# First narrow attention of a four-layer kernel: shares applied to the outputs, shift of the scores on GpSimd, scores waiting bank by bank

## The chip, the cores and the metric

One core of one Trainium2 chip. The metric is the device time of one execution in microseconds (us), the median over runs; smaller is better. Engines: TensorE (PE, with its weight loads PEld), VectorE (DVE), ScalarE (ACT), GpSimd (POOL), SyncE (SP). Each works through its own instructions in order and meets the others at semaphores.

## What is computed

Four layers on x (2 x 1024 x 256, float32), each a gated cross-attention to a context of 77 rows per batch and a gated feed-forward part. The change touches the attentions of layers 2 and 3, with 16 heads of 16 columns. What layer 2 computes, cut from the reference:

```python
def _L2_xattn_ref(values, keys, queries, mask, Wv, Wk, Wq, Wo, bo):
    ...
    energy = jnp.einsum('nqhd,nkhd->nhqk', q, k)
    energy = jnp.where(mask == 0, jnp.float32(-1e+20), energy)
    attention = jax.nn.softmax(energy / np.sqrt(EMBED).astype(np.float32), axis=3)
    out = jnp.einsum('nhql,nlhd->nqhd', attention, v).reshape(N, q_len, EMBED)
    return out @ Wo.T + bo
```

Layer 3 computes the same without a mask and with biases on queries, keys and values. Layers 0 and 1 have wider heads and their own functions (pe_wide and its like).

## The kernel before

Tiles are of 128 rows of x, NT = 16 of them. A tile's scores are 128 x 1232 (16 heads x 77 context rows) and fill three banks of PSUM; two such sets alternate, and so do two buffers prob in SBUF. The stage of layer 2 is called with n = 5 ("attention 5" below), that of layer 3 with n = 6 ("attention 6"). Both go through pe_attention, act_attention, dve_attention and pool_attention, one function for each engine, each a loop over the tiles t in program order. Only the order inside each engine's function and the semaphores set the order of the work.

One tile of attention 5, by its steps:
- TensorE: scores (L727) once the turned and normalised tile is copied; it also waits for p_kept, the copies of the probabilities of tile t-2, since these lie in the same banks.
- VectorE: adds the mask's bias (L922, PSUM to prob), maximum of each head (dve_softmax, L613), subtracts it (L615, semaphore shifted), then after_shift(): the tile t+2 is normalised (L267), residuals of two earlier tiles are added (L900) on odd t, their statistics (L910) are taken on even t. Then it waits for powered, sums (L620) and takes the reciprocal (L623, semaphore shares_made).
- ACT: exp (L860, semaphore powered); copies of the turned probabilities (L844, L847), of the turned tile (L825), and of the weighed outputs of a pair of tiles (keep_outputs, L835).
- GpSimd: multiplies the probabilities by the reciprocals (L983, semaphore weights_made), then adds the gated bias to x (L985). after(t) follows: pool_root at t = 4, 8, 12, 15 (L243 and what follows it), and pool_order at t = 12. Ahead of its first tile stands pool_group_rows of the stage before (L2144 to L2152).
- TensorE again: turns the probabilities (L395) after weights_made, weighs the values by pairs of tiles (L742, function weigh), and multiplies by the output weights (L751, function outputs). weigh(u) also waits for the residuals of the pair before, because they use the same bank.

At t = 2 of attention 5, before(t) on VectorE handles four tiles of the stage before ("gated rows", L1962, two inputs in SBUF, each followed by L1965), ahead of the normalisation. At the end of attention 5 the rows for the next stage are fed: dve_feed_rows (L267), pe_feed_turn, act_feed_copy (L1634), pe_feed_product (L1627) and the tables (L2304, L2309 and after), and the first experts' matrices follow.

Attention 6 already does it otherwise. It has no bias, VectorE reads the scores from PSUM, and the reciprocals are not multiplied into the probabilities: GpSimd spreads them over 256 columns (L990), TensorE turns them (L382), ACT copies them (keep_shares, L856), and VectorE multiplies the weighed outputs of a pair by them (divided_outputs, L905). There TensorE also makes the queries (L712), which ACT copies (L830).

Of the kernel before, what the change touches and what calls it, by code (L numbers as in the profile page):

```python
# [64 lines left out]
def build(nc, ctx, a, out):  # L65
# [313 lines left out]
    def pe_turn_shares(pe, t):  # L379
        pe.wait_ge(weights_made, 6 * NT + t + 1)  # L380
        for g in range(KD):
            ins = pe.transpose(shares_bank(t)[:, g * P:(g + 1) * P],  # L382
                               wide_shares[:, t % 2, :, :].rearrange("p h c -> p (h c)")[:, g * P:(g + 1) * P], ident[:, :])
        return ins

    def pe_turn_probabilities(pe, n, t):
        g, base = NT * n + t, t % 2 * 3 * BANK
        if n == 6:
            pe.wait_ge(powered, g + 1)
        else:  # L390
            pe.wait_ge(weights_made, g + 1)
        for b0 in range(0, CH, 4):
# [4 lines left out]
            if n == 6 and t >= 1 and b0 + 4 >= CH:  # L397
                ins = pe_turn_shares(pe, t - 1)
# [209 lines left out]
    def dve_softmax(dve, n, t, src, after_shift, divide=True):  # L608
# [4 lines left out]
        dve.tensor_reduce(negmax, src, AX.X, ALU.max, negate=True).then_inc(dve_step, 1)  # L613
        dve.wait_ge(dve_step, vs())
        dve.tensor_tensor(Pb, src, negmax.unsqueeze(2).to_broadcast([P, H, S2]), ALU.add).then_inc(shifted, 1)  # L615
        after_shift()
        dve.wait_ge(powered, g + 1)
        if n == 6 and t >= 2:
            dve.wait_ge(weights_made, g - 1)
        dve.tensor_reduce(total, Pb, AX.X, ALU.add).then_inc(dve_step, 1)  # L620
        dve.wait_ge(dve_step, vs())
        if not divide:
            dve.reciprocal(total, total).then_inc(shares_made, 1)  # L623
            return
# [44 lines left out]
    wide_shares = prep[:, 8704:9216].rearrange("p (n h c) -> p n h c", n=2, c=HD)  # L669
    shares_T = prep[:, 7680:8704].rearrange("p (n g i q) -> p n g i q", n=2, g=KD, i=2)  # L670
# [25 lines left out]
    def pe_attention(pe, n, wo, w_query=None, feed=False):  # L696
# [19 lines left out]
        def scores(t):  # L716
# [5 lines left out]
            if t >= 2:  # L722
                pe.wait_ge(p_kept, 3 * (g0 + t - 1))
            for bank in NARROW:
# [7 lines left out]
        def weigh(u, halves=(0, 1)):  # L732

            bt, turned_pair, bank = 2 * u // TB, pair_probT[u % 2], weighed_bank(u)
            if halves[0] == 0:
                pe.wait_ge(p_kept, 3 * (g0 + 2 * u + 2))
# [33 lines left out]
        for t in range(NT):  # L770
# [5 lines left out]
            if feed:  # L776
# [6 lines left out]
                if t == NT - 2:  # L783
                    pe_feed_turn(pe, 0)
                    pe.wait_ge(p_kept, 3 * (g0 + t + 1))
# [32 lines left out]
    def act_attention(act, n, scale, q_bias=None, feed=False):  # L818
# [14 lines left out]
        def keep_outputs(u):  # L833
            act.wait_ge(weighed, g0 + 2 * u + 2)
            act.copy(outT[:, :, :].rearrange("p g c -> p (g c)"), weighed_bank(u)).then_inc(outputs_kept, 1)  # L835

        def keep_probabilities(t):
# [3 lines left out]
            for b0 in range(0, CH, 4):  # L841
                m = min(4, CH - 1 - b0)
                act.wait_ge(p_turned, 3 * (g0 + t) + b0 // 4 + 1)
# [2887 lines left out]
```

## Time and profile before

| | |
|---|---|
| median of 3 runs | 3222.62 us (3219.43 to 3229.44) |
| the profiled execution | 3226.4 us, span 3225.1 us |
| busy share of the span | PE 94%, PEld 69%, DVE 66%, ACT 38%, POOL 26% |
| attention 5 | about 2024.5 to 2163 us of the span |
| attention 6 | about 2420 to 2549 us of the span |
| granted TensorE clock, mean | 0.978 of full speed |

Times in the rows are microseconds from the start of the span, and durations in microseconds unless a row says otherwise. A timeline row with x2 or more holds neighbouring instructions of the same kind, with the time of all of them; in square brackets stands the idle time before it and what ended it. The busy share of TensorE comes from pipelined matmuls, so 94% doesn't mean that it works at its peak.

### The profile page before, as it was taken

The numbers are of one execution on the slowest core, as the hardware profiler recorded it, in microseconds if no ns is written. First come the engines' busy times: TensorE is split into PE (matmuls) and PEld (weight loads), VectorE is DVE, ScalarE is ACT, GpSimd is POOL, SyncE is SP. The second block draws the span as 40 slices with busy tenths as digits, with TensorE's granted clock in tenths as the row PEclk, the third lists the DMA queues.
The fourth block names the chain that finished last, engine by engine and source line by source line (L and its number), as shares of the span: only waits on it lengthen the run. The fifth ranks groups of instructions, "written<-read, shape, count | busy, mean of one in ns | idle before, by whom it ended". The sixth has DMA issues, their size and how long they took to land.

```text
span 3225.1 us, 43512 instructions
## 1 busy us (share of the span) xinstructions
PE 3036.0 (94%) x16352; PEld 2228.9 (69%) x16352; DVE 2137.6 (66%) x3877; ACT 1224.5 (38%) x2349; POOL 850.8 (26%) x1286
## 2 busy tenths in 40 slices
PE   7999999999999999999999999789999899997996
PEld 5678877667767776777699999565666655555664
DVE  5996879567855885686478887883228667764113
ACT  4343332553355335432233333331225345662331
POOL 1306500100110020001246655440443221111554
PEclk9999999999999999999999999999999999997998
DMA  5200100010002000200032221002550011112633
GB/s 137 67 1 1 29 27 1 13 42 27 1 14 68 0 1 14 67 1 1 14 92 79 87 85 53 20 1 105 211 198 1 21 34 51 33 39 103 217 124 108
DMA packets 104614, 176.42 MB, mean 55 GB/s; under 512 B 27125, under 2 KB 75799, under 8 KB 99671
## 3 DMA queue, kind: packets, MB, share of 16 engines
q1 hardware_dynamic: 89527, 102.32, 10.2%
q0 software_dynamic: 14880, 71.33, 6.2%
q8 instruction: 132, 2.16, 0.3%
q14 instruction: 75, 0.61, 0.1%
HBM read 198.31 MB, written 17.56 MB: 67 GB/s over the span
## 4 chain that ended last, share of the span: by engine, by line
PE 75%; DVE 13%; ACT 4%; issue 3%; POOL 2%; DMA 2%; SPq 0%; DVEq 0%; ACTq 0%; POOLq 0%
PE psum L419 9%; PE psum L442 8%; PE psum L1393 7%; PE psum L1405 6%; PE psum L2527 6%; PE psum L1874 5%; PE psum L1829 5%; PE psum L2548 3%; PE psum L409 2%; PE psum L455 2%; PE psum L1114 2%; PE psum L2703 2%; PE psum L3128 2%; DVE row L620 1%; DVE psum L3386 1%
## 5 line engine op out<-in xcount | busy, mean ns | idle before, releaser
L419 PE MATMUL psum<-Vt,shared 128*128 128x256 f32 (+1 forms) x1600 | 361.7, 381 | 0.4
L442 PE MATMUL psum<-Kt,xnTt 128*128 128x512 f32 (+1 forms) x960 | 343.9, 508 | 0.5 <-ACT xnTt L527 0.5
L419 PEld LDWEIGHTS psum<-Vt,shared 128*128 128x128 f32 (+1 forms) x1600 | 297.8, 190 | 39.3 <-issue 1.2
L442 PEld LDWEIGHTS psum<-Kt,xnTt 128*128 128x128 f32 x960 | 179.9, 190 | 158.0 <-issue 153.1
L1405 PEld LDWEIGHTS psum<-expert_w,prep 128*128 128x128 f32 x1024 | 194.6, 190 | 77.7 <-issue 57.4
L245 POOL TENSOR_SCALAR root_v<-meanvar 128x8 f32<-128x8 f32 (+3 forms) x19 | 8.6, 455 | 903.7 <-DVE meanvar L223 903.7
L3386 DVE CUSTOM_DVE_ANT_0 psum<-psum,expert_w 128x128 f32<-128x128 f32 (+7 forms) x256 | 191.8, 775 | 76.5 <-PE psum L3128 73.3
L1405 PE MATMUL psum<-expert_w,prep 128*128 128x256 f32 x1024 | 240.8, 379 | 0.0
L1393 PE MATMUL psum<-weights,expert_w 128*128 128x512 f32 x512 | 240.3, 593 | 0.0
L1319 DVE SCALAR_TENSOR_TENSOR bias<-Kt,small,bias 128x1232 f32<-128x1232 f32 x96 | 149.1, 1554 | 129.8 <-ACT Kt L1303 128.5
L620 DVE TENSOR_REDUCE row<-shared 128x16 f32<-128x1232 f32 x112 | 160.5, 1433 | 81.5 <-ACT shared L536 70.0
L3275 ACT ACTIVATE prep<-psum 128x512 f32<-128x512 f32 (+3 forms) x384 | 167.2, 493 | 108.0 <-PE psum L3151 107.1
L2620 DVE TENSOR_TENSOR prep<-psum,prep 128x512 f32<-128x512 f32 x62 | 42.8, 691 | 210.3 <-PE psum L2527 193.7
L1448 ACT ACTIVATE prep<-psum,bias 128x512 f32<-128x512 f32 x128 | 88.0, 688 | 237.2 <-PE psum L1393 237.2
L536 ACT ACTIVATE shared<-shared 128x1232 f32<-128x1232 f32 x80 | 98.5, 1232 | 186.8 <-DVE shared L615 186.8
L647 DVE TENSOR_TENSOR shared<-psum,bias 128x1232 f32<-128x1232 f32 x80 | 115.0, 1437 | 70.5 <-PE psum L442 65.4
L1393 PEld LDWEIGHTS psum<-weights,expert_w 128*128 128x128 f32 x512 | 96.1, 190 | 69.1 <-issue 63.1
L615 DVE TENSOR_TENSOR shared<-shared,row 128x1232 f32<-128x1232 f32 x96 | 140.9, 1467 | 3.3
L613 DVE TENSOR_REDUCE row<-shared 128x16 f32<-128x1232 f32 x96 | 137.8, 1436 | 3.3
L527 ACT COPY xnTt<-psum 128x256 f32<-128x256 f32 x80 | 29.3, 374 | 288.1 <-PE psum L365 288.1
L1303 ACT ACTIVATE Kt<-fside,small 128x1232 f32<-128x1232 f32 x96 | 134.4, 1403 | 1.5 <-DVE bias L1319 1.5
L3128 PE MATMUL psum<-weights 72*128 72x512 bf16 (+3 forms) x384 | 106.8, 335 | 19.8 <-DVE row L3386 17.1
(510 smaller groups left out, 6636.5 us busy)
## 6 DMA issues: line engine op xcount, KB each, us to landing
weights<-in_L_ffn_w SPq DMA_DIRECT2D x32, 512.0 KB, 4.7
expert_w<-in_L_ffn_w SPq DMA_DIRECT2D x32, 512.0 KB, 4.5
expert_w<-in_L_xattn_Wf SPq DMA_DIRECT2D x16, 512.0 KB, 5.9
weights<-q_parts SPq DMA_DIRECT2D x32, 144.0 KB
weights<-k_parts SPq DMA_DIRECT2D x96, 48.0 KB
weights<-in_L_xattn_Wk SPq DMA_DIRECT2D x4, 1024.0 KB, 4.9
weights<-in_L_xattn_Wv SPq DMA_DIRECT2D x4, 1024.0 KB, 7.0
weights<-in_L_xattn_Wq SPq DMA_DIRECT2D x4, 1024.0 KB, 5.3
```

Of the source, the lines that this page charges most:

```text
L419: ins = pe.matmul(o_bank(t), probT[0:rows, t % 2, c, :], Vt[0:rows, t // TB, c, :], start=(c == 8), stop=(c == 7))
L442: ins = pe.matmul(flat[:, par * 3 * BANK + at:par * 3 * BANK + at + cols], xnTt[:, par, k, :], Kt[:, t // TB, k, src:src + cols], start=(k ...
L620: dve.tensor_reduce(total, Pb, AX.X, ALU.add).then_inc(dve_step, 1)
L1319: dve.scalar_tensor_tensor(flat_bias, hinge[:, j % 2, :], wto[:, j:j + 1], flat_bias, ALU.mult, ALU.add).then_inc(hinge_added, 1)
L1393: ins = pe.matmul(bank, slot(s)[0][:, k, f * P:(f + 1) * P], xnT_of(g)[:, k, :], start=(k == 0), stop=(k == KD - 1))
L1405: ins = pe.matmul(y[:, t * D:(t + 1) * D], hidden[:, n % 4, t * P:(t + 1) * P], slot(s)[2][:, f, :], start=(n % GROUP_STEPS == 0 and t % 2 ...
L1829: return pe.matmul(product_of(i), lhs, rhs, start=start, stop=stop, skip_group_check=True)
L1874: ins = pe.matmul(acc_of(i)[:, t * P:(t + 1) * P], lhs[:, t * P:(t + 1) * P], rhs, start=(begin and start and t == 0), stop=end, skip_grou ...
L2527: ins = pe.matmul(psum[:, 2 * (c % 2) + n, :], rows_xT[:, c % 2, k, :], w[:, at:at + F], start=(k == 0), stop=(k == KD - 1))
L3128: ins = pe.matmul(flat[:, base + at:base + at + w], heads[0:STACK, 0, s, t * P:(t + 1) * P], heads[0:STACK, 1, s, at:at + w], start=True, ...
L3275: act.activation(expT[:, h % 2, to:to + w], psum[:, ring_bank(("piece", h, i)), 0:w], ACT.Exp, scale=float(HD3) ** -0.5).then_inc(exp_made, 1)
L3386: dve.tensor_tensor_reduce(flat[:, base:base + cols], flat[:, base:base + cols], later[:, S - cols:S], 1.0, -3.0e38, ALU.add, ALU.max, max ...
```

## The change

Attention 5 takes over the way of attention 6 for the shares: no multiplication of the probabilities; the reciprocals are spread, turned, copied, and multiplied into the outputs of a pair by VectorE. On ACT, keep_outputs goes, keep_shares comes. TensorE turns the probabilities after powered. VectorE's L615 goes from attention 5, and GpSimd does the shift, signalled by the maximum over the semaphore row_made, which counts two per tile in attention 5 (maximum and reciprocal). In both attentions TensorE's scores wait bank by bank for the copied chunks of tile t-2 and no longer once for all three. The shares of attention 5 lie in a part of Vt that is free by then. tiles_turned(n, t) counts the turns and copies of the tiles before t: three per tile, and one more behind attention 5's last tile. The diff, cut:

```diff
@@ pe_turn_shares, pe_turn_probabilities @@
-        if n == 6:
-            pe.wait_ge(powered, g + 1)
-        else:
-            pe.wait_ge(weights_made, g + 1)
+        pe.wait_ge(powered, g + 1)
...
-            if n == 6 and t >= 1 and b0 + 4 >= CH:
-                ins = pe_turn_shares(pe, t - 1)
+            if t >= 1 and b0 + 4 >= CH:
+                ins = pe_turn_shares(pe, n, t - 1)
@@ dve_softmax @@
-        dve.tensor_reduce(negmax, src, AX.X, ALU.max, negate=True).then_inc(dve_step, 1)
-        dve.wait_ge(dve_step, vs())
-        dve.tensor_tensor(Pb, src, negmax.unsqueeze(2).to_broadcast([P, H, S2]), ALU.add).then_inc(shifted, 1)
+        if n == 5:
+            dve.tensor_reduce(negmax, src, AX.X, ALU.max, negate=True).then_inc(row_made, 1)
+        else:
+            dve.tensor_reduce(negmax, src, AX.X, ALU.max, negate=True).then_inc(dve_step, 1)
+            dve.wait_ge(dve_step, vs())
+            dve.tensor_tensor(Pb, src, negmax.unsqueeze(2).to_broadcast([P, H, S2]), ALU.add).then_inc(shifted, 1)
         after_shift()
         dve.wait_ge(powered, g + 1)
-        if n == 6 and t >= 2:
+        if n >= 5 and t >= 2:
             dve.wait_ge(weights_made, g - 1)
...
+    def tiles_turned(n, t):
+
+        return 3 * (NT * n + t) + n - 5
@@ pe_attention @@
-            if t >= 2:
-                pe.wait_ge(p_kept, 3 * (g0 + t - 1))
-            for bank in NARROW:
+            for i, bank in enumerate(NARROW):
+                if t >= 2:
+                    pe.wait_ge(p_kept, tiles_turned(n, t - 2) + i + 1)
...
         if feed:
             pe_tables(pe)
-        else:
-            pe_turn_shares(pe, NT - 1).then_inc(p_turned, 1)
+            pe.wait_ge(xt_fed, 2)
+        pe_turn_shares(pe, n, NT - 1).then_inc(p_turned, 1)
         weigh(PAIRS - 1)
         if feed:
             pe_feed_turn(pe, 2)
-            pe.wait_ge(xt_fed, 2)
         outputs(PAIRS - 1)
@@ act_attention @@
-        def keep_outputs(u):
-            act.wait_ge(weighed, g0 + 2 * u + 2)
-            act.copy(outT[:, :, :].rearrange("p g c -> p (g c)"), weighed_bank(u)).then_inc(outputs_kept, 1)
...
-                    if not feed and t >= 1:
+                    if t >= 1:
                         ins = keep_shares(t - 1)
@@ dve_attention, after_shift @@
                 before(t)
                 if biased:
+                    if t % 2 == 0 and t >= 4:
+                        divided_outputs(t // 2 - 2)
                     if t + 2 < NT:
                         dve_normed(dve, n, x, t + 2)
                     if t % 2 and t >= 5:
                         residual(t - 5)
                         residual(t - 4)
+                    if t == NT - 1:
+                        divided_outputs(PAIRS - 2)
...
         for u in range(PAIRS - 3 if biased else PAIRS - 2, PAIRS):
-            if not biased:
+            if not biased or u == PAIRS - 1:
                 divided_outputs(u)
@@ pool_attention @@
             if n == 5:
-                pool.wait_ge(shares_made, NT * (n - 5) + t + 1)
-                pool.tensor_tensor(Pb, Pb, shares.to_broadcast([P, H, S2]), ALU.mult).then_inc(weights_made, 1)
+                Pb = prob[:, par, :].rearrange("p (h c) -> p h c", h=H)
+                pool.wait_ge(row_made, 2 * t + 1)
+                pool.tensor_tensor(Pb, Pb, negmax.to_broadcast([P, H, S2]), ALU.add).then_inc(shifted, 1)
             pool.wait_ge(normed, NT * n + t + 1)
             pool.tensor_tensor(x[:, t, :], x[:, t, :], gated_bo, ALU.add).then_inc(bo_added, 1)
-            if n == 6:
-                pool.wait_ge(shares_made, NT * (n - 5) + t + 1)
-                if t >= 2:
-                    pool.wait_ge(p_turned, 3 * (NT * n + t))
-                pool.tensor_copy(wide_shares[:, par, :, :], shares.to_broadcast([P, H, HD])).then_inc(weights_made, 1)
+            pool.wait_ge(row_made, 2 * t + 2 if n == 5 else 2 * NT + t + 1)
+            if t >= 2:
+                pool.wait_ge(p_turned, tiles_turned(n, t))
+            pool.tensor_copy(wide_shares(n)[:, par, :, :], shares.to_broadcast([P, H, HD])).then_inc(weights_made, 1)
             if after:
                 after(t)
```

## Rows read from the trace of the kernel before

**Rows 1.** Page, part 1: busy us (share of the span) and instructions per engine.
```profile
PE 3036.0 (94%) x16352; PEld 2228.9 (69%) x16352; DVE 2137.6 (66%) x3877; ACT 1224.5 (38%) x2349; POOL 850.8 (26%) x1286
```

**Rows 2.** Chain of waits in attention 5: start us, us, what.
```profile
2097.23 2.26 POOL shared L983
...
2101.55 1.26 ACT shared L860
...
2102.84 1.45 DVE row L620
```

**Rows 3.** Timeline, tiles 14 and 15 of attention 5: start us, us, engine, line, operation.
```profile
2139.73 1.44 DVE L620 TENSOR_REDUCE row<-shared 128x16 f32<-128x1232 f32 x1
...
2141.20 0.25 DVE L623 RECIPROCAL row<-row 128x16 f32<-128x16 f32 x1
2141.37 1.38 DVE L922 TENSOR_TENSOR shared<-psum,bias 128x1232 f32<-128x1232 f32 x1
2141.53 2.25 POOL L983 TENSOR_TENSOR shared<-shared,row 128x1232 f32<-128x1232 f32 x1 [4.42 <-DVE row L623]
2142.78 1.44 DVE L613 TENSOR_REDUCE row<-shared 128x16 f32<-128x1232 f32 x1
...
2144.25 1.51 DVE L615 TENSOR_TENSOR shared<-shared,row 128x1232 f32<-128x1232 f32 x1
...
2145.69 0.86 DVE L900 SCALAR_TENSOR_TENSOR x<-psum,tanh_g,x 128x256 f32<-128x256 f32 x2
```

**Rows 4.** Busy time by stretches, mid-stage: us, each engine's busy us, PEclk, DMA.
```profile
2059.00:2133.84 74.84, 59.89 (x416) 39.52 (x414) 70.71 (x87) 31.90 (x65) 39.27 (x47) 1.00 0.00 1
```

**Rows 5.** Waits in attention 6: engine, line, releaser: us in total, times, longest.
```profile
PE psum L727 <- ACT prep L856: 6.0, 7, 1.0
```

**Rows 6.** Timeline, the first three tiles of attention 5.
```profile
2033.25 2.36 POOL L2152 TENSOR_TENSOR prep<-prep,fside 128x1024 f32<-128x1024 f32 x1
...
2034.79 1.38 DVE L922 TENSOR_TENSOR shared<-psum,bias 128x1232 f32<-128x1232 f32 x1
...
2047.08 0.47 DVE L1962 SCALAR_TENSOR_TENSOR x<-prep,gates,x 128x256 f32<-128x256 f32 x1
...
2052.81 1.38 DVE L922 TENSOR_TENSOR shared<-psum,bias 128x1232 f32<-128x1232 f32 x1
```

**Rows 7.** Timeline, one odd tile of attention 6.
```profile
2477.66 0.40 DVE L267 TENSOR_SCALAR xn<-x,meanvar,rstd 128x256 f32<-128x256 f32 x1
...
2480.69 0.69 DVE L905 TENSOR_TENSOR prep<-psum,prep 128x512 f32<-128x512 f32 x1
...
2480.89 1.24 ACT L844 COPY prep<-psum 128x512 f32<-128x512 f32 x3
...
2481.48 0.38 PE L365 MATMUL psum<-ident,xn 128*128 128x128 f32 x2
...
2482.69 2.36 PE L727 MATMUL psum<-Kt,qTt 128*128 128x512 f32 x8 [0.83 <-ACT prep L856]
```

**Rows 8.** Timeline, the end of attention 5.
```profile
2146.70 2.32 PE L742 MATMUL psum<-shared,Vt 128*32 128x256 f32 x34 [1.55 <-DVE x L900]
...
2148.78 2.58 DVE L267 TENSOR_SCALAR inner<-x,meanvar,rstd 128x256 f32<-128x256 f32 x2
2148.94 2.26 POOL L983 TENSOR_TENSOR shared<-shared,row 128x1232 f32<-128x1232 f32 x1 [4.47 <-DVE row L623]
```

**Rows 9.** Line 2149 over the whole run: duration ns min/median/max, first and last start us.
```profile
L2149 POOL TENSOR_TENSOR prep<-expert_w x4: 731/734/1927, 1733.4 to 2030.5; 128x256 f32<-128x256 f32 x4
```

**Rows 10.** Timeline of GpSimd after tile 12 of attention 5.
```profile
2129.78 1.30 POOL L243 TENSOR_SCALAR root_v<-meanvar 128x4 f32<-128x4 f32 x1
...
2133.52 0.29 POOL L2227 TENSOR_SCALAR_AFFINE_SELECT small<-ones 128x128 f32<-128x128 f32 x1
```

**Rows 11.** Two stretches of attention 5, columns as in group 4.
```profile
2044.00:2045.00 1.00, 0.00 (x0) 0.00 (x0) 0.96 (x2) 0.00 (x0) 1.00 (x1) 1.00 0.00 0
2048.00:2049.00 1.00, 1.00 (x2) 0.48 (x3) 0.97 (x4) 0.93 (x1) 0.00 (x0) 0.50 0.00 0
```

More of the change, by code:

```diff
@@ L622, in dve_softmax @@
         if not divide:
-            dve.reciprocal(total, total).then_inc(shares_made, 1)
+            dve.reciprocal(total, total).then_inc(row_made, 1)
             return
@@ L668, in build, with wide_shares, shares_T @@
     HD = D // H
-    wide_shares = prep[:, 8704:9216].rearrange("p (n h c) -> p n h c", n=2, c=HD)
-    shares_T = prep[:, 7680:8704].rearrange("p (n g i q) -> p n g i q", n=2, g=KD, i=2)
+    def wide_shares(n):
+        at = flat_V1[:, 3840:4352] if n == 5 else prep[:, 8704:9216]
+        return at.rearrange("p (n h c) -> p n h c", n=2, c=HD)
+    def shares_T(n):
+        at = flat_V1[:, 2816:3840] if n == 5 else prep[:, 7680:8704]
+        return at.rearrange("p (n g i q) -> p n g i q", n=2, g=KD, i=2)
+    def tiles_turned(n, t):
+        return 3 * (NT * n + t) + n - 5
     def shares_bank(t):
@@ L735, in weigh @@
             if halves[0] == 0:
-                pe.wait_ge(p_kept, 3 * (g0 + 2 * u + 2))
+                pe.wait_ge(p_kept, tiles_turned(n, 2 * u + 2))
                 if u >= 1 and u < PAIRS - 1:
@@ L855, in keep_shares @@
                 act.wait_ge(outputs_kept, PAIRS * (n - 5) + u - 1)
-            return act.copy(shares_T[:, u % 2, :, t % 2, :], shares_bank(t).rearrange("p (g q) -> p g q", g=KD))
+            return act.copy(shares_T(n)[:, u % 2, :, t % 2, :], shares_bank(t).rearrange("p (g q) -> p g q", g=KD))
         def power(t):
@@ L876, in act_attention @@
                 keep_tile(t + 3)
-            if feed and t % 2 == 0 and t >= 2:
-                keep_outputs(t // 2 - 1)
             if q_bias is not None and t + 3 < NT:
@@ L883, in act_attention @@
                     act_feed_copy(act, i)
+        act.wait_ge(p_turned, tiles_turned(n, NT) + 1)
+        keep_shares(NT - 1).then_inc(p_kept, 1)
         if feed:
-            keep_outputs(PAIRS - 1)
             for i in range(2, FEED_PAIRS):
                 act_feed_copy(act, i)
-        else:
-            act.wait_ge(p_turned, 3 * (g0 + NT) + 1)
-            keep_shares(NT - 1).then_inc(p_kept, 1)
     def dve_attention(dve, n, biased, gate, before, after, feed=False):
@@ L903, in divided_outputs @@
             dve.wait_ge(weighed, g0 + 2 * u + 2)
-            dve.wait_ge(p_kept, 3 * (g0 + 2 * u + 2) + (3 if u < PAIRS - 1 else 1))
+            dve.wait_ge(p_kept, tiles_turned(n, 2 * u + 2) + (3 if u < PAIRS - 1 else 1))
             dve.tensor_tensor(outT[:, :, :].rearrange("p g c -> p (g c)"), weighed_bank(u),
-                              shares_T[:, u % 2, :, :, :].rearrange("p g i q -> p (g i q)"), ALU.mult).then_inc(outputs_kept, 1)
+                              shares_T(n)[:, u % 2, :, :, :].rearrange("p g i q -> p (g i q)"), ALU.mult).then_inc(outputs_kept, 1)
         def statistics(t):
@@ L918, in dve_attention @@
             if t >= 2:
-                dve.wait_ge(p_turned, 3 * (g0 + t - 1))
+                dve.wait_ge(p_turned, tiles_turned(n, t - 1))
             if biased:
@@ L971, in dve_attention @@
                 dve_tables(dve)
-    shares_made = sem("shares_made")
+    row_made = sem("row_made")
     def pool_attention(pool, n, gated_bo, after=None):
@@ L978, in pool_attention @@
             par = t % 2
-            Pb = prob[:, par, :].rearrange("p (h c) -> p h c", h=H)
-            shares = row[:, par, H:2 * H].unsqueeze(2)
+            negmax, shares = (row[:, par, i * H:(i + 1) * H].unsqueeze(2) for i in range(2))
             if n == 5:
-                pool.wait_ge(shares_made, NT * (n - 5) + t + 1)
-                pool.tensor_tensor(Pb, Pb, shares.to_broadcast([P, H, S2]), ALU.mult).then_inc(weights_made, 1)
+                Pb = prob[:, par, :].rearrange("p (h c) -> p h c", h=H)
+                pool.wait_ge(row_made, 2 * t + 1)
+                pool.tensor_tensor(Pb, Pb, negmax.to_broadcast([P, H, S2]), ALU.add).then_inc(shifted, 1)
             pool.wait_ge(normed, NT * n + t + 1)
             pool.tensor_tensor(x[:, t, :], x[:, t, :], gated_bo, ALU.add).then_inc(bo_added, 1)
-            if n == 6:
-                pool.wait_ge(shares_made, NT * (n - 5) + t + 1)
-                if t >= 2:
-                    pool.wait_ge(p_turned, 3 * (NT * n + t))
-                pool.tensor_copy(wide_shares[:, par, :, :], shares.to_broadcast([P, H, HD])).then_inc(weights_made, 1)
+            pool.wait_ge(row_made, 2 * t + 2 if n == 5 else 2 * NT + t + 1)
+            if t >= 2:
+                pool.wait_ge(p_turned, tiles_turned(n, t))
+            pool.tensor_copy(wide_shares(n)[:, par, :, :], shares.to_broadcast([P, H, HD])).then_inc(weights_made, 1)
             if after:
```

10 lines of the change are left out of this document (5 added, 5 removed).

## The prediction

> **What bounds the kernel now.** I read the page first (shares and slices), then the chain of waits over the two narrow attentions, then the timeline of single tiles in them. The page has TensorE busy 94% of the span [rows 1], so only a stage where TensorE is not the last to arrive can be moved by work on other engines. The first narrow attention (attention 5) is such a stage. Its chain of waits goes round once a tile without touching TensorE for long: GpSimd's multiplication, transposes and copies, exp of the next tile, row sum, reciprocal, and GpSimd again; transposes and copies have the 2.06 us between 2099.49 and 2101.55 [rows 2]. VectorE is nearly full besides: in one tile [rows 3] bias add 1.38, maximum 1.44, shift 1.51, then 0.40 of normalising or its like and 0.86 of residuals, sum 1.44, reciprocal 0.25, together 7.3 us; over ten tiles it was busy 70.71 of 74.84 us, 94% [rows 4]. Two limits of the same size, so taking away one alone gives nothing.
>
> The second narrow attention (attention 6) is bound by TensorE. The waits list shows TensorE's scores waiting 6.0 us in 7 pieces for ACT's copy of the shares (L856) [rows 5]: the second thing that the change can move.
>
> **What the change does in attention 5, per tile.** Call T the end of the maximum L613. Removed: VectorE's shift (1.51) and GpSimd's multiplication by the shares. Added on GpSimd: the shift, 128x1232 in place with a row of 16 broadcast, which is the shape of the multiplication it replaces, so 2.25 us [rows 3]. Its other end is the plain two-tensor add L2152, 2.36 us for 1024 columns [rows 6], so 2.84 for 1232; I take 2.25, since shape and broadcast are the same, and nothing there suggests less. GpSimd also makes the widened shares (a copy of 256 columns, put at 0.4 to 0.5), VectorE multiplies outputs once a pair (0.69, L905) [rows 7], TensorE turns the shares, two transposes a tile, and ACT copies them instead of the outputs.
>
> What matters is the order on VectorE, which has one queue. dve_softmax still does maximum, after_shift(), wait for powered, sum. Before, shift and after_shift work filled VectorE, and only exp (1.26) had to be covered. Now exp(t) waits for GpSimd's shift(t), and VectorE can't go to tile t+1 meanwhile. From T to the sum: hand-over 0.08 (as from L623 at 2141.20+0.25 to L983 at 2141.53), shift 2.25, exp 1.26, and hand-overs of 0.05 and 0.03 (as from exp's end at 2102.81 to the sum at 2102.84): 3.67 us [rows 2, 3]. Then sum to next bias add 1.48 + 0.17, and bias add to T 1.41 + 1.44 (starts at 2139.73, 2141.20, 2141.37, 2142.78) [rows 3]. **New period 3.67 + 1.65 + 2.85 = 8.17 us a tile**, all serial, against (2141.37 - 2052.81)/12 = 7.38 [rows 3, 6].
>
> Everything else of the change lies in the 3.67 us in which VectorE waits. On odd tiles that is a norm of 0.40 [rows 7] and two residuals 0.86; on even ones the divided outputs 0.69, a norm and two statistics of about 0.4 each. In even tiles the norm comes while GpSimd's shift is running, and the trace shows what that does: two norms of 2.58 us (L267, 2148.78) beside a GpSimd multiplication from 2148.94 to 2151.20 [rows 8], against about 0.7 for two. The second waited until GpSimd was done. So the norm ends at T+2.5 and the statistics at T+3.3, still under 3.67. If this cover failed (0.4 us more in it), the tile would grow by what is over.
> The Trainium skill, SBUF — State Buffer, section "SBUF: two separate sides", says that a VectorE instruction in a two-port mode or with two SBUF inputs and a GpSimd instruction hold a shared port pair exclusively, the other blocking fully; the trace agrees (2.58 us above). Without such a lock tile 2 below would cost 1.85 us less and the forecast would fall by that.
>
> TensorE was busy 59.89 of the 74.84 us [rows 4], 11.8 us a pair of tiles; four more transposes, about 0.5 us, make 12.3 of the new 16.3, so it follows. In the new order it waits for the norm of an even tile (T+2.5) and has an idle stretch of about 3 us each pair.
>
> **The sum for attention 5**, in the trace's own times.
> - Tile 0. GpSimd's shift stands behind pool_group_rows, which ends with L2152 at 2033.25+2.36 = 2035.6. One of its adds, L2149, took 1.93 against a median of 0.73 [rows 9] (it ran beside the VectorE shift L615, which is gone), so the queue is free at 2034.4. Shift to 2036.7, exp to 2038.0, then 0.03+1.48+0.17: bias add of tile 1 at 2039.7, where it was at 2034.79 [rows 6]. **+4.9**. Before, VectorE's shift did not care about this queue.
> - Tiles 1 and 2. Tile 1 takes 8.17 (2047.9), T of tile 2 is 2050.7. There before() runs the gated rows (L1962, two SBUF inputs, four times). From the first of them to the next bias add it is 5.73 us (2052.81 - 2047.08) [rows 6]; GpSimd's shift gets in after the first one and holds the second back: ready at T+0.86, free at T+2.7, 1.85 more. Bias add of tile 3 at 2058.3 against 2052.81: **+5.5** up to here.
> - Tiles 3 to 14: 12 x 8.17 = 98.0 against 88.6: **+9.5**.
> - GpSimd's roots, in after(t) at t = 4, 8 and 12, stand between the widened shares and the next shift. At t = 12 root and order take from 2129.78 to 2133.81, of which L243 has 1.30 where about 0.2 is usual (it met a VectorE shift) [rows 10], so 3.0; with 0.5 for the copy before it, it ends 3.5 after the reciprocal, and the shift is wanted at 2.85: 0.65 late. The shorter ones 0.15 each: **+1.0**. They had 4.4 us of slack before.
> - Tail. The residuals that weigh(6) waits for follow the maximum at once, 1.5 us sooner than before (L900 at 2145.69, L742 at 2146.70) [rows 3, 8], but the last division on VectorE stands behind three sets of feed rows, a root and dve_tables, so outputs(7) come at about the same distance from T as they did. The wait for xt_fed 2 moves ahead of the last shares and weigh(7), but pe_feed_product(1), before it in TensorE's order, has waited for the same value: nothing. Ahead of weigh(6) TensorE now idles some 4 us and may find a lower clock: 0 to +3.5, I take **+1**.
> Together 5.5+9.5+1.0+1 = **+17**.
>
> **Attention 6.** scores(t+2) now wait bank by bank. On odd t TensorE has nothing between the turned tile (L365, until 2481.86) and the scores L727 at 2482.69, although the first copy L844 (from 2480.89, about 0.6) was done at 2481.5 [rows 7]. The first bank's matmuls then take 0.9 us, by which the second copy is there, and the third bank comes after 1.9 us, when the shares' copy is long over. So each 0.83 to 0.97 goes. The next in line, exp and norm, have a microsecond and more. 7 of them are **-6**; bounds 0 (another wait steps in) and -7. In attention 5 the same wait (0.92 per tile) goes as well and is worth nothing there, since TensorE isn't last.
>
> Net +17 - 6 = +11. The profiled execution took 3226.4 us, which gives 3237.4; the median of the three runs is 3222.6, 3.8 lower, so **3233.6**.
>
> **Rivals.**
> 1. *VectorE's relief counts* (faster). If VectorE's busy time were the limit, a tile would lose 1.51 and gain 0.35 (0.69 a pair): that is 15 x 1.16 = 17 us off, and with attention 6 -23: 3199. For it: VectorE was 94% busy [rows 4]. Against: it decides by whether VectorE has 3.67 us of work between maximum and sum; it has 1.3 to 1.9. Break-even with the old 7.38 is at 2.88, which GpSimd's 2.25 alone plus exp exceeds. 0.06.
> 2. *Bank by bank gives nothing in attention 6*: 3222.6 + 17 = 3240. It needs TensorE to be held by the query copy or exp instead. 0.12.
> 3. *GpSimd's add is dear*: 2.84 instead of 2.25, 15 x 0.59 = +9: 3242. 0.10.
> The Trainium skill, GPSIMD Engine Reference, section 4.1 "Engine selection", speaks against this change: two-input elementwise work is about 2x slower on GpSimd than on VectorE. That would be 2 x 1.51 = 3.0 us, an estimate by this page, for +11 more (3245); the multiplication row has 2.25, which is 1.5x, and so far the trace does not agree.
> 4. *The clock of TensorE falls in attention 5.* After TensorE idled from 2042.7 to 2045.2, the granted clock went to 0.50 (1.2 GHz), and was there at 2048 to 2049 [rows 11]. The new idle stretch of 3 us per pair is like it. At half clock every TensorE step takes twice as long; by my schedule seven microseconds of that per pair leave the scores 0.7 us ahead of VectorE, and three more would make each of 7 pairs 1.5 us longer: +10, 3244. 0.13.
> 5. *A kinder clock later*: the stage's last part and the expert stage after it begin at half clock, and another timing could spare about 5 us: 3228. 0.11.
> The likeliest, the sum as reckoned, 0.48: 3229 to 3238.
>
> **Chances.** 0.3% is about what a measurement of this kernel can tell from no change: 9.7 us, so the line is at 3232.3, just under the forecast. Of the likeliest case I put 0.30 above it and 0.18 below. Slower 0.30 + 0.12 + 0.10 + 0.13 = 0.65; same 0.18 + 0.11 = 0.29; faster 0.06. The range goes from the kinder clock less 2 us to the dear end of rivals 3 and 4: 3226 to 3246; left out are rival 1 and the cases where two dear ones meet.
>
> **What would show it.** In the profile after: bias add to bias add (the former L922) 8.1 to 8.3 us in mid-stage; VectorE's sum preceded by 1.5 to 2.3 us of idle released by ACT on odd tiles and by little on even ones; the chain of waits as VectorE, GpSimd, ACT, VectorE; GpSimd's shift at 2.25; a norm of over 2 us in even tiles; the first shift near 2034.5; in attention 6 no wait of L727 for L856, and the stage 6 us shorter. The prediction is wrong if the period stays below 7.6, if the shift takes over 2.5, or if TensorE's rows in attention 5 are doubled for long.

## The result, and the profile after

The changed kernel takes 3231.68 us (median of 19 runs, 3225.48 to 3235.29) where the kernel before, run beside it, takes 3223.06 (19 runs, 3215.46 to 3232.89). The ratio is 1.0027, with a 95% interval of 1.0019 to 1.0035: 8.6 us slower, where 11.0 were forecast. The sign is sure; the size is just under the line of 0.3% above which the prediction called the change slower, and the interval reaches over that line. The profiled execution took 3231.02 us against 3226.4 before. In this section I read it by stages, since what attention 5 lost and attention 6 gave back are both larger than the net.

Page of the kernel after, part 1 (busy us, share of the span, instructions):

```profile
PE 3034.7 (94%) x16384; PEld 2232.7 (69%) x16384; DVE 2126.9 (66%) x3869; ACT 1223.3 (38%) x2357; POOL 852.2 (26%) x1302
```

Beside [rows 1] VectorE has 10.7 us less to do and GpSimd 1.4 us more. Nothing in this view tells that the kernel became slower. The timeline of two tiles in mid-stage does (kernel after; VectorE, GpSimd and ACT; start us, us, engine, line, operation, and in brackets the idle time before it and what ended it):

```profile
2098.27 1.44 DVE L620 TENSOR_REDUCE row<-shared 128x16 f32<-128x1232 f32 x1 [2.61 <-ACT shared L865]
2099.74 0.25 DVE L623 RECIPROCAL row<-row 128x16 f32<-128x16 f32 x1
...
2099.91 1.38 DVE L923 TENSOR_TENSOR shared<-psum,bias 128x1232 f32<-128x1232 f32 x1
...
2101.33 1.44 DVE L611 TENSOR_REDUCE row<-shared 128x16 f32<-128x1232 f32 x1
...
2102.68 0.68 DVE L906 TENSOR_TENSOR prep<-psum,Vt 128x512 f32<-128x512 f32 x1
...
2102.84 2.25 POOL L988 TENSOR_TENSOR shared<-shared,row 128x1232 f32<-128x1232 f32 x1 [2.38 <-DVE row L611]
...
2103.28 1.96 DVE L267 TENSOR_SCALAR xn<-x,meanvar,rstd 128x256 f32<-128x256 f32 x1
...
2105.12 1.23 ACT L865 ACTIVATE shared<-shared 128x1232 f32<-128x1232 f32 x1 [3.01 <-POOL shared L988]
2105.16 0.74 DVE L911 BATCH_NORM_STATS2 bn<-x 128x6 f32<-128x256 f32 x2
...
2106.39 1.44 DVE L620 TENSOR_REDUCE row<-shared 128x16 f32<-128x1232 f32 x1
...
2108.02 1.38 DVE L923 TENSOR_TENSOR shared<-psum,bias 128x1232 f32<-128x1232 f32 x1
```

From one bias add (L923) to the next it is 8.11 us (2099.91 to 2108.02), where [rows 3, 6] gave 7.38. The maximum L611 ends at 2102.77, the row sum L620 starts at 2106.39: 3.62 us, filled by GpSimd's shift (2.25) and ACT's exp (1.23) one behind the other. VectorE has one queue, and the sum stands in it ahead of the next tile's bias add. The sum of the tile before (2098.27) shows the same from the other side: VectorE idle for 2.61 us until exp was done. The chain of waits of the kernel after, one tile earlier (tile 7), is the whole round, with hand-overs of 0.07 us and less between the engines (start us, us, what):

```profile
2091.70 1.39 DVE shared L923
...
2093.12 1.45 DVE row L611
...
2094.63 2.35 POOL shared L988
...
2097.01 1.24 ACT shared L865
...
2098.27 1.45 DVE row L620
```

Over twelve tiles, in the columns of [rows 4]:

```profile
2058.90:2158.00 99.10, 82.60 (x545) 58.18 (x543) 78.10 (x97) 38.91 (x86) 47.53 (x64) 0.92 0.00 1
```

VectorE is busy 78.10 of 99.10 us, 79%, where it was 94%. The waits list of attention 5 (kernel after, 2025 to 2180; engine, line, releaser: us in total, times, longest) says who keeps whom:

```profile
ACT shared L865 <- POOL shared L988: 57.7, 16, 8.7
...
DVE row L620 <- ACT shared L865: 30.5, 12, 7.2
```

ACT's exp waits for the shift in all 16 tiles, and VectorE's sum for exp in 12 of them; for TensorE's scores VectorE waits in tile 0 alone, as in the kernel before.

The start of the stage, where the forecast saw the largest single loss (kernel after, timeline):

```profile
2033.14 2.35 POOL L2156 TENSOR_TENSOR prep<-prep,fside 128x1024 f32<-128x1024 f32 x1
2035.45 2.25 POOL L988 TENSOR_TENSOR shared<-shared,row 128x1232 f32<-128x1232 f32 x1
...
2038.99 1.44 DVE L620 TENSOR_REDUCE row<-shared 128x16 f32<-128x1232 f32 x1 [7.19 <-ACT shared L865]
...
2040.63 1.38 DVE L923 TENSOR_TENSOR shared<-psum,bias 128x1232 f32<-128x1232 f32 x1
...
2051.77 2.42 POOL L988 TENSOR_TENSOR shared<-shared,row 128x1232 f32<-128x1232 f32 x1 [2.39 <-DVE row L611]
...
2052.46 2.01 DVE L1966 SCALAR_TENSOR_TENSOR x<-prep,gates,x 128x256 f32<-128x256 f32 x1
```

The first shift stands behind the group rows (L2156) and starts at 2035.45; VectorE waits 7.19 us. In tile 2 the second gated row (L1966) takes 2.01 instead of 0.47 [rows 6], until the shift that began before it is done.

In attention 6 the wait of [rows 5] is gone from the waits list. The odd tile's scores now start as soon as TensorE has turned the normed tile, before the copy of the shares (L861) has begun (kernel after, timeline):

```profile
2482.13 0.38 PE L365 MATMUL psum<-ident,xn 128*128 128x128 f32 x2
...
2482.35 2.29 PE L737 MATMUL psum<-Kt,qTt 128*128 128x512 f32 x8
...
2482.73 0.39 ACT L861 COPY prep<-psum 128x256 f32<-128x256 f32 x1
```

The account, from the starts of the same instructions in the two traces (us, after less before):

| stretch | before | after | change |
|---|---|---|---|
| bias add of tile 0 to that of tile 3 | 25.88 | 30.88 | +5.0 |
| bias add of tile 3 to that of tile 15 | 88.56 | 98.89 | +10.3 |
| bias add of tile 15 to the copy of the logits | 32.25 | 30.34 | -1.9 |
| the experts, up to attention 6's first maximum | 251.18 | 251.70 | +0.5 |
| attention 6, up to the next stage's first norm | 124.51 | 118.44 | -6.1 |

The sum is +7.8. Attention 5 began 1.1 us later in this execution, and 4.3 us came back behind attention 6, where nothing was changed (granted clock from 2585 to 2625: 0.83 before, 0.96 after; that the clock is the whole reason is not shown). So the spans differ by 4.7, and the medians by 8.6.

### The profile page after: what moved, and what is told of

Same layout as the page of the kernel before. It is cut to its first block, busy times and chain, and to the rows that moved or that the text cites. A ratio compares the mean times of both kernels' runs of the same rounds, so it can differ in the third digit from the quotient of the medians.

```text
span 3229.8 us, 43628 instructions
## 1 busy us (share of the span) xinstructions
PE 3034.7 (94%) x16384; PEld 2232.7 (69%) x16384; DVE 2126.9 (66%) x3869; ACT 1223.3 (38%) x2357; POOL 852.2 (26%) x1302
## 4 chain that ended last, share of the span: by engine, by line
PE 74%; DVE 14%; issue 4%; ACT 3%; POOL 3%; DMA 1%; SPq 0%; DVEq 0%; POOLq 0%; ACTq 0%
PE psum L416 9%; PE psum L439 8%; PE psum L1397 7%; PE psum L1409 6%; PE psum L2531 6%; PE psum L1878 5%; PE psum L1833 5%; PE psum L2552 3%; PE psum L406 2%; PE psum L452 2%; PE psum L1118 2%; PE psum L2707 2%; DVE row L620 2%; PE psum L3132 2%; DVE psum L3390 1%
## 5 line engine op out<-in xcount | busy, mean ns | idle before, releaser
L620 DVE TENSOR_REDUCE row<-shared 128x16 f32<-128x1232 f32 x112 | 160.5, 1433 | 106.3 <-ACT shared L533 70.0
L533 ACT ACTIVATE shared<-shared 128x1232 f32<-128x1232 f32 x80 | 98.5, 1232 | 187.0 <-DVE shared L615 187.0
L579 ACT COPY shared<-psum 128x512 f32<-128x512 f32 (+1 forms) x240 | 107.4, 482 | 42.9 <-PE psum L406 42.3
L615 DVE TENSOR_TENSOR shared<-shared,row 128x1232 f32<-128x1232 f32 x80 | 116.3, 1454 | 2.8
```

## Experiments

The theory: in attention 5 the new period is one serial round, VectorE, GpSimd, ACT and VectorE again, closed by VectorE's fixed order; the bank-wise wait is a gain of its own in attention 6; the shares on the outputs cost next to nothing. The rivals: TensorE or its clock sets the new period, or the shares do, or the two gains and losses don't simply add.

**One wait instead of three.** The changed kernel, with its scores waiting once for all the copies of the tile's bank:

```
+            if t >= 2:
+                pe.wait_ge(p_kept, tiles_turned(n, t - 2) + 3)
-            for i, bank in enumerate(NARROW):
-                if t >= 2:
-                    pe.wait_ge(p_kept, tiles_turned(n, t - 2) + i + 1)
+            for bank in NARROW:
```

> The changed kernel, but the scores wait once for all three copies of tile t-2, as before. Theory (the serial chain costs attention 5 some 14 us, the waits by bank return 6 in attention 6): the waits of L727's successor for the shares' copy are back in attention 6, 6 us in 7 pieces; attention 6 is 6 us longer than in the changed kernel and like before; attention 5 stays at 8.17 a tile; in all 6 us slower than the changed kernel, 13 to 15 us slower than the kernel before. Rival (waits by bank give nothing in attention 6 and the measured time comes from a smaller loss in attention 5): no difference from the changed kernel, 8 to 9 us slower than before.

Measured: 3237.20 us, ratio to the kernel before 1.0042 (1.0027 to 1.0058), by the medians 14.6 us slower. This interval overlaps that of the changed kernel, so the stage has to show it: attention 6 is back at 124.31 us. Its waits list has the old row again, and the odd tile's scores wait as in [rows 7] (kernel with one wait; waits, then timeline):

```profile
PE psum L737 <- ACT prep L861: 6.0, 7, 1.0
```

```profile
2485.82 2.36 PE L737 MATMUL psum<-Kt,qTt 128*128 128x512 f32 x8 [0.83 <-ACT prep L861]
```

The steps of attention 5 are those of the changed kernel (12.61, 8.21, 10.06, ...). So the wait is worth 6 us in attention 6 and nothing in attention 5.

**The banks alone.** The kernel before, with only the waits by bank:

```
-            if t >= 2:
-                pe.wait_ge(p_kept, 3 * (g0 + t - 1))
-            for bank in NARROW:
+            for i, bank in enumerate(NARROW):
+                if t >= 2:
+                    pe.wait_ge(p_kept, 3 * (g0 + t - 2) + i + 1)
```

> The kernel before with one edit: scores wait bank by bank in both attentions, nothing else. Theory: 6 us faster than before, all of it in attention 6; attention 5 unchanged at 7.38 us a tile, since TensorE is not last there. Rival (the copies are waited for elsewhere next): within 1 us of before.

Measured: 3213.13 us, ratio 0.9972 (0.9961 to 0.9983). Attention 6 takes 118.44 us, the same as in the changed kernel to the hundredth; attention 5 keeps the steps of before, but for one tile (8.03 for 7.41) in which the granted clock fell to 0.50. That is 9.5 us by the medians where the stage gives 6.1; the ratio's interval, 5.5 to 12.6 us, holds both. The two profiled executions are 15.6 us apart, and most of that lies where the code is the same: 3.1 in the end of attention 5, 4.1 in the experts, 3.6 behind attention 6. Whether the edit has a part in these is not shown. For the end of attention 5, 29.13 us from the last bias add to the logits instead of 32.25, the windows show a reason (the kernel before, then banks alone, columns as in [rows 4]; the last but two is the granted clock):

```profile
2169.00:2172.00 3.00, 3.00 (x17) 3.00 (x16) 0.00 (x0) 0.59 (x1) 0.00 (x0) 0.50 0.00 0
```

```profile
2169.00:2172.00 3.00, 3.00 (x28) 3.00 (x28) 0.11 (x1) 1.05 (x2) 0.00 (x0) 1.00 0.02 5
```

From about 2165 to 2182 the one ran at 0.50 (1.2 GHz), the other at 1.00 (2.4 GHz).

**The shift back on VectorE.** The changed kernel with the shares on the outputs and the banks, without the shift on GpSimd:

```
-        if n == 5:
-            dve.tensor_reduce(negmax, src, AX.X, ALU.max, negate=True).then_inc(row_made, 1)
-        else:
...
+        dve.tensor_reduce(negmax, src, AX.X, ALU.max, negate=True).then_inc(dve_step, 1)
+        dve.wait_ge(dve_step, vs())
+        dve.tensor_tensor(Pb, src, negmax.unsqueeze(2).to_broadcast([P, H, S2]), ALU.add).then_inc(shifted, 1)
```

> The changed kernel with the shift of attention 5 back on VectorE; shares stay applied to the outputs. Theory (the loss is the serial link through GpSimd, not the shares): mean of an odd tile 2.85+1.51+1.3+1.65 = 7.3 and an even one 2.85+1.51+1.9+1.65 = 7.9 at most, so 7.3 to 7.6 a tile instead of 8.2, and tile 0's 4.9 us are back; attention 5 about 13 us shorter than in the changed kernel, within 3 us of before; with attention 6 at -6, 3 to 8 us faster than before. Rival (the shares' extra transposes, copies and divisions cost the time): stays near 8.2 a tile and 8 us slower than before.

Measured: 3217.03 us, ratio 0.9986 (0.9974 to 0.9998). The period falls to 7.26 on most tiles and 7.45 to 7.85 on the others, 7.45 in the mean of the last eleven steps against 7.38 before. The place of the long wait is filled (this kernel, timeline):

```profile
2103.72 1.44 DVE L612 TENSOR_TENSOR shared<-shared,row 128x1232 f32<-128x1232 f32 x1
2105.08 0.41 DVE L267 TENSOR_SCALAR xn<-x,meanvar,rstd 128x256 f32<-128x256 f32 x1
2105.41 0.87 DVE L898 SCALAR_TENSOR_TENSOR x<-psum,tanh_g,x 128x256 f32<-128x256 f32 x2
2106.46 1.44 DVE L617 TENSOR_REDUCE row<-shared 128x16 f32<-128x1232 f32 x1 [0.19 <-ACT shared L862]
```

Only exp has to be waited out, and VectorE's own work covers it but for 0.19 us. From the first bias add of attention 5 to the last it is 116.44 us, against 129.77 in the changed kernel and 114.44 before. So of the 15.3 us that the change loses there, 13.3 go with the shift on GpSimd, and 2.0 stay with everything else, the shares on the outputs among it. With the shift undone the change is faster than before, by 5.5 us of the medians.

**The next tile's lead put ahead of the wait.** If it is VectorE's order that closes the round, then bias add and maximum of tile t+1, issued before VectorE waits for exp of tile t, open it, with GpSimd still making every shift:

```
+        if n == 5 and t + 1 < NT:
+            lead(t + 1)
         dve.wait_ge(powered, g + 1)
...
+        def lead(t):
...
+            dve.tensor_tensor(Pb, src, bias[:, t, :].unsqueeze(1).to_broadcast([P, H, S2]), ALU.add).then_inc(dve_step, 1)
+            dve.wait_ge(dve_step, vs())
+            dve.tensor_reduce(row[:, par, 0:H], Pb, AX.X, ALU.max, negate=True).then_inc(row_made, 1)
...
+            if n == 5 and t + 1 < NT:
+                shift(t + 1)
```

(`shift` is GpSimd's wait and its add, made now before it spreads the shares of tile t.)

> The changed kernel, but in attention 5 VectorE makes bias add and maximum of tile t+1 before it waits for tile t's exp, and GpSimd shifts tile t+1 before it spreads the shares of tile t. Nothing is added or left out. Theory (the loss is only that VectorE stands idle over GpSimd's shift and exp): the idle time is filled, VectorE's own work sets 6.1 to 6.3 us a tile, or TensorE a little more (6.3 to 6.7); 15 tiles by 1.7 = 25 us less than the changed kernel, and 3 to 5 more from tile 0's queue: 14 to 22 us faster than before. Rival (GpSimd's or TensorE's work is the limit, or the shared port, VectorE's norms waiting for the shift): 7.4 to 8.2 a tile, not faster than before.

Measured: 3204.65 us, ratio 0.9945 (0.9930 to 0.9959), 18 us below the kernel before and faster than every version without the lead. From tile 4 on the period is 6.1 to 6.4 us (6.7 in the last); the first four tiles take 33.7 us together, 33.2 before. VectorE in one tile, and the stage's windows (kernel with the lead ahead):

```profile
2095.33 0.93 DVE L267 TENSOR_SCALAR xn<-x,meanvar,rstd 128x256 f32<-128x256 f32 x1
2096.18 0.86 DVE L903 SCALAR_TENSOR_TENSOR x<-psum,tanh_g,x 128x256 f32<-128x256 f32 x2
2096.96 1.43 DVE L924 TENSOR_TENSOR shared<-psum,bias 128x1232 f32<-128x1232 f32 x1
2098.42 1.44 DVE L926 TENSOR_REDUCE row<-shared 128x16 f32<-128x1232 f32 x1
2099.77 1.43 DVE L622 TENSOR_REDUCE row<-shared 128x16 f32<-128x1232 f32 x1
...
2103.26 1.44 DVE L924 TENSOR_TENSOR shared<-psum,bias 128x1232 f32<-128x1232 f32 x1 [0.24 <-PE psum L739]
```

```profile
2058.00:2128.00 70.00, 67.81 (x495) 47.47 (x494) 66.07 (x90) 36.25 (x80) 43.22 (x61) 1.00 0.01 1
```

The sum L622 (2099.77) is that of the tile whose maximum was L926 one period earlier; exp has long been done and nothing is waited for. VectorE is 94% busy again, TensorE 97%, and it is TensorE's scores that VectorE waits for now (0.24 us at 2103.26). GpSimd's shift takes what it took (same kernel, timeline):

```profile
2093.86 2.25 POOL L999 TENSOR_TENSOR shared<-shared,row 128x1232 f32<-128x1232 f32 x1 [3.01 <-DVE row L926]
```

**A longer link.** A GpSimd copy of 192 columns before each shift, once in the changed kernel and once in the one with the lead ahead. In a serial round it must show in full, in an open one not. (With the lead ahead the copy also waits for the shift of the tile before, which GpSimd, working in order, has behind it by then.)

```
+    spare = sb("spare", [P, 192])
...
+                pool.tensor_copy(spare[:, :].rearrange("p (h c) -> p h c", h=H), negmax.to_broadcast([P, H, 12]))
```

> The changed kernel with one more small GpSimd copy (128x192, some 0.35 us with its gap, result unused) between the wait for the maximum and the shift of each tile of attention 5. Theory (maximum, shift, exp and sum are one serial chain): every tile grows by the copy, 8.17 to about 8.5, and attention 5 by 14 to 16 times 0.35, 5 to 6 us; about 14 us slower than before. Rival (VectorE's own work or TensorE sets the tile): no change against the changed kernel, since GpSimd is half idle.

> The same extra copy ahead of GpSimd's shift, put into the version in which VectorE runs a tile ahead. Theory (there the chain through GpSimd has slack, since VectorE has work for the whole of shift and exp): 0 to 1 us in attention 5 against that version, though the copy is the same as in the run before; from its rows the shift ends 1.2 us or more before ACT needs it on most tiles. Rival (GpSimd is on the critical path there as well): 5 to 6 us.

Measured, changed kernel with the copy: 3231.52 us, ratio 1.0039 (1.0021 to 1.0056). From the first bias add to the last it is 134.62 us instead of 129.77, +4.85. The copy stands between the maximum and the shift (this kernel, timeline):

```profile
2103.21 0.35 POOL L989 COPY spare<-row 128x192 f32<-128x192 f32 x1 [2.37 <-DVE row L611]
2103.52 2.25 POOL L990 TENSOR_TENSOR shared<-shared,row 128x1232 f32<-128x1232 f32 x1
```

Every step has grown by about 0.3 (8.40 for 8.11, 8.52 for 8.21). One has grown by 0.75 (tile 3, 8.96 for 8.21): its exp stood behind ACT's copies of what TensorE had turned late, after a stretch at a granted clock of 0.50. That is the serial round, link by link. By medians alone this can't be told: the kernel is 9.6 us slower than before, where about 14 were expected, the ratio is 1.2 thousandths above that of the changed kernel, and the intervals overlap.

With the lead ahead: 3207.06 us, ratio 0.9959 (0.9943 to 0.9974). Here the expectation missed. The stage grew by 4.2 us from first to last bias add (102.39 to 106.6) where the round's slack should have swallowed nearly all. 1.4 of it is one step (tile 3, 9.46 for 8.02), and that is the clock, not the link: TensorE's 22 matmuls that only keep it at work, ahead of that tile's turning, took 4.90 us instead of 3.81 and the turning 1.64 instead of 1.26, since the granted clock was still at 0.50 (until 2060 here, until 2055 in the other; lead ahead, then with the copy):

```profile
2052.42 3.81 PE L371 MATMUL psum<-ident 128*128 128x128 f32 x22
```

```profile
2054.29 4.90 PE L371 MATMUL psum<-ident 128*128 128x128 f32 x22
```

Of the other 2.8 us, tiles 1 and 2 have 0.3 each and eight of the last eleven tiles 0.23 to 0.29 each, and one instruction shows where from (lead ahead with the copy; compare 2095.33 above, the same tile without it):

```profile
2098.29 2.25 POOL L1002 TENSOR_TENSOR shared<-shared,row 128x1232 f32<-128x1232 f32 x1
```

```profile
2099.47 1.22 DVE L267 TENSOR_SCALAR xn<-x,meanvar,rstd 128x256 f32<-128x256 f32 x1
```

The norm ended at 2100.69, behind the end of the shift (2100.54) by 0.15; without the copy it ended at 2096.26, behind 2096.11 by the same 0.15. Every norm of tiles 3 to 13 ends 0.15 to 0.17 behind the shift, in both kernels. A shift that ends 0.3 later holds VectorE's norm 0.3 longer, though nobody needs the shift yet. The round is open for the data, but not for whatever holds the two engines apart.

**Tile 0's shift on VectorE.** The forecast put +4.9 on tile 0, since the first shift stands behind the group rows on GpSimd:

```
+            if t == 0:
+                dve.wait_ge(row_made, 1)
+                dve.tensor_tensor(Pb, src, negmax.unsqueeze(2).to_broadcast([P, H, S2]), ALU.add).then_inc(shifted, 1)
```

> The changed kernel with the shift of tile 0 alone on VectorE, as before the change. Theory (tile 0's shift stands behind the stage before on GpSimd's queue, 4.9 us by the prediction, 12.60 against 7.86 us from the first bias add to the second in the traces): the first step is 7.9 again, all later ones stay at 8.2; attention 5 is 4.7 us shorter than in the changed kernel, 3 to 4 us slower than before. Rival (the delay would come back at the next tile, whose shift meets the same queue): less than 2 us gained.

> The version in which VectorE runs a tile ahead, and tile 0's shift on VectorE besides. Theory: exp of tile 0 comes at about 6 us after the first bias add and not 10; the scores of tile 2, for which VectorE waited 3.2 us, come as much earlier; 3 to 4 us less in attention 5 than without, so 20 to 22 us faster than before. Rival (GpSimd's queue holds tile 1's shift instead, or the 4 gated rows take the gain): within 1 us of the version without.

Measured, in the changed kernel: 3225.83 us, ratio 1.0012 (1.0003 to 1.0022). First to last bias add 125.25 us, 4.52 less than in the changed kernel; the first step is 7.85 as before, 4.7 less, and the others stay (8.21, 10.06, 8.11) but for the fourth (8.46 for 8.21). That is the queue's price, alone. By the medians the kernel is 3.9 us slower than before, as expected (3 to 4).

Measured, with the lead ahead: 3203.28 us, ratio 0.9934 (0.9921 to 0.9948). This missed what the theory gave it: the stage is 0.5 us shorter (101.88 for 102.39), not 3 to 4. Exp of tile 0 did end early, 6.2 us after the first bias add. But the second bias add comes 5.58 us after the first where it was 3.69, since the shift stands ahead of it on VectorE, and the third, 15.11 us after the first where it was 16.15, had to wait (this kernel, TensorE and VectorE):

```profile
2033.93 4.90 PE L371 MATMUL psum<-ident 128*128 128x128 f32 x22
2038.62 1.71 PE L392 MATMUL psum<-ident,shared 128*128 128x128 f32 x10
...
```

```profile
2042.84 1.44 DVE L924 TENSOR_TENSOR shared<-psum,bias 128x1232 f32<-128x1232 f32 x1 [3.38 <-PE psum L739]
```

The 22 matmuls that only keep TensorE at work (L371, from pe_stay_at_work) took 4.90 us; for tile 0 of the changed kernel and of the one with the lead ahead they took 2.62. Here they began later, behind a norm that stood behind the shift on VectorE, after TensorE had done 0.56 us of work in 4, and ran at half clock (this kernel, windows):

```profile
2030.00:2034.00 4.00, 0.56 (x3) 0.56 (x4) 3.96 (x4) 1.23 (x1) 3.90 (x4) 0.84 0.00 0
2034.00:2038.50 4.50, 4.50 (x23) 4.50 (x23) 4.43 (x5) 0.37 (x1) 4.44 (x3) 0.50 0.21 25
```

So tile 0 was turned from 2038.62, behind them in TensorE's order, 10.9 us after the first bias add, where GpSimd's late shift had it at 11.0 (2037.12 less 2026.11). What VectorE had won, TensorE no longer had, and the scores of tile 2 (L739) had VectorE wait 3.38 us. The time of the two kernels can't be told apart (intervals 0.9921 to 0.9948 and 0.9930 to 0.9959).

## Why the prediction was right

The sign, the place and the mechanism were right; the sum came out 2.4 us high by the medians, and 3.7 high by the stages of the two traces (11.0 for 7.3), of which the tail has 2.9. The chances did less well: the prediction gave 0.65 to a ratio above its line of 0.3%, with its forecast 1.3 us over that line, and the measured 0.27% lies under it.

*The period.* Forecast 8.17, measured 8.11 on even tiles and 8.21 on odd ones from tile 3 on, where no root stands before the shift. Each link is where it was put: shift 2.25, exp 1.23, hand-overs of 0.07, 0.03 and 0.04. The 0.10 of the odd tiles is a thing the forecast didn't have: VectorE's norm of 0.40 is still running when the shift begins, and the shift takes 2.35 (2094.63 in the chain above). The argument that removing VectorE's 1.51 buys nothing, since VectorE has to wait for what took its place, is what the shift on VectorE (7.45) and the lead ahead (6.1) show from two sides. The idle before the sum on odd tiles is 2.6 to 3.4 us, not 1.5 to 2.3. That range doesn't follow from the prediction's own terms, which leave 2.4 (0.40 and 0.86 of 3.67); nor does the work of up to 1.9 us that its first rival gives VectorE there.

*Start of the stage.* +5.5 forecast, +5.0 measured: tile 0 is +4.7 (forecast 4.9), by the kernel with tile 0's shift on VectorE 4.5; the first shift was due at 2034.5 and began at 2035.45, in a stage that began 1.1 late. The second gated row (L1966) was held to 2.01, 1.5 us more where 1.85 were forecast, and tile 2 took no longer than before (10.07 for 10.05): VectorE's own shift of 1.51 is gone from it, and the length of the gated rows hides GpSimd's shift and exp.

*Roots.* +1.0 forecast. The steps behind them are those of the odd tiles 5, 9 and 13, 8.36, 8.36 and 8.86 against 8.21 on odd tiles without a root: 0.15, 0.15 and 0.65, each as forecast. Tiles 3 to 14 came to 98.89 us where period and roots together gave 99.0.

*Norm beside the shift.* 1.96 us in even tiles (a pair of them 2.04 at 2153.71) instead of 0.40, and covered: it ends at 2105.24, exp at 2106.35. The cover is thin where statistics are gathered as well: VectorE was idle ahead of the sum for 0.49 us in tile 6, but for 0.07 in tiles 8 and 12. The Trainium skill, SBUF — State Buffer, section "SBUF: two separate sides", says that a VectorE instruction in a two-port mode, or with two SBUF inputs, blocks until a GpSimd instruction that started first is done, and the other way round. The traces agree here, in the 0.93 and 1.22 of the lead-ahead kernels and in the 2.35 of the odd tiles' shift; that the norm is in such a mode no run shows.

*The price of GpSimd's add.* 2.25, so the rival of 2.84 is out. The Trainium skill, GPSIMD Engine Reference, section 4.1 "Engine selection", has two-input work at about twice VectorE's time; the trace has 2.25 against 1.44 to 1.51, 1.5 to 1.6 times, and the measurement decides.

*Attention 6.* -6 forecast, -6.1 measured, and given back by one wait to within 0.2. The eight kernels that wait by bank have 118.4 to 120.5 us there, the two that wait once 124.3 and 124.5.

*The tail.* This is the term that was off: +1 forecast, -1.9 measured. What was foreseen did happen. TensorE idled 3.87 us ahead of weigh(6) and came back slower (kernel after, timeline; 2.32 us in [rows 8]):

```profile
2161.58 3.16 PE L752 MATMUL psum<-shared,Vt 128*32 128x256 f32 x34 [3.87 <-DVE x L901]
```

But the kernel before had itself run at 0.50 from 2165 to 2182, where the kernel after was at full clock from 2166 to 2186 and at 0.50 from 2187 to 2197, behind nearly all of the tail (the logits are copied at 2188.14). Against the instructions of before at full clock (29.13 in the kernel with the banks alone) the changed kernel's 30.34 is +1.2; the same code took 32.49 in the kernel with one wait and 31.73 in that with tile 0's shift on VectorE, +3.4 and +2.6. So what the change does to the tail lies within the 0 to +3.5 of the forecast. The term came out at -1.9 because the execution of before, which it is set against, was itself 3.1 us longer in this stretch than the same code at full clock. That is chance, near to what the prediction listed as a rival of its own (kinder clock, 3228).

*Clock in attention 5* (rival 4). It did fall: the mean over the twelve tiles is 0.92, where it was 1.00, and one stretch was wholly at 0.50:

```profile
2088.00:2093.00 5.00, 4.03 (x11) 3.21 (x12) 4.48 (x6) 1.49 (x2) 1.90 (x3) 0.50 0.00 0
```

It cost nothing: the waits list has VectorE waiting for the scores once, for 5.6 us, and that is tile 0's, as before the change. TensorE was busy 82.60 of 99.10 us even so. The condition of the rival came true only in part: in these twelve tiles the clock was at 0.50 four times, for 3.4 to 6.8 us, and not for some ten microseconds of every pair, which is what its price needed.

Still open is why the granted clock falls when it does. The traces show it at 0.50 in stretches of 3 to 17 us in different places of the same code, and no kernel here was made to hold it. Nor was the contention between the norm and the shift taken out of a kernel; the two copies only measured it.

## To carry over

When work goes from a full engine to an idle one, draw the round it now makes and ask what stands in the first engine's queue behind the wait: here a relief of 1.5 us became an idle of 2.6 to 3.4 on every other tile, and the engine's share of busy time, 94% before and 79% after, was no measure of what it had to win. The same hand-over, with its companions, paid 12 us in the stage once the next tile's lead was put ahead of the wait, so look at the order on the waiting engine together with the work that leaves it. And where two changes come in one, measure each alone: the half that gained here (-6 in attention 6, 0.9972 by itself) was hidden by the half that lost.

## What the runs showed of the hardware

- A GpSimd instruction holds up a VectorE norm by its end, not by its length alone: the norm took 0.93 us where the shift ended at 2096.11 and 1.22 where it ended 0.29 later in relation to it, with 0.15 us between the two ends both times; a gated row with two SBUF inputs ended 0.28 behind (2054.47 and 2054.19). Slack in the data flow doesn't help there. It works the other way too: a shift that began while a norm of 0.40 was running took 2.35 instead of 2.25.
- From the last bias add of attention 5 to the logits the same instructions took 32.25 us in the kernel before and 29.13 with the banks alone, and those of the change 30.34, 31.73 and 32.49 in three kernels. The granted clock stood at 0.50 in other places each time; 2 to 3 us of a stage come and go between kernels that are alike there.
- A GpSimd copy of 192 columns took 0.34 to 0.35 us and one of 256 columns 0.40; the shift of 1232 took 2.25 where neither a norm nor a gated row was running on VectorE at its start, and up to 2.35 and 2.42 where one was.
- The 22 matmuls that only keep TensorE at work took 2.62 us at full clock and 4.90 at half clock, and the turning of the tile stands behind them. Whether the kernels would be faster without them was not tried.
